# The variance of an encoder's second normalisation: both chunks of squares through TensorE instead of one summed chunk

## What is computed

```python
o = attention(x) @ Wo[l].T + bo[l]
x = _ln(x + o, ln1_g[l], ln1_b[l])
ff = jax.nn.gelu(x @ W1[l].T + b1[l], approximate=False) @ W2[l].T + b2[l]
x = _ln(x + ff, ln2_g[l], ln2_b[l])
# _ln: m = mean(x); v = mean((x - m) ** 2); (x - m) * rsqrt(v + eps) * g + b
```

## Time and profile before

| | |
|---|---|
| median of 3 runs | 932.23 us (931.94, 932.23, 936.35) |
| profiled execution | 932.26 us |
| its span | 930.5 us |
| mean granted TensorE clock | 0.959 of 2.4 GHz |
| encoder loop (five layers) | about 442 to 820 us of the span |

### The profile page before, as it was taken

One profiled execution on the slowest core, in us unless ns is written; L12 is line 12 of the kernel. 1 busy time (PEld: TensorE's weight loads), 2 busy tenths in 40 slices (PEclk: granted clock), 3 DMA queues, 4 the chain that ended last, 5 costly groups with the idle time before them and its releaser, 6 DMA issues.

```text
span 930.5 us, 16226 instructions
## 1 busy us (share of the span) xinstructions
PE 839.1 (90%) x5890; PEld 765.4 (82%) x5890; DVE 661.7 (71%) x1298; ACT 458.1 (49%) x788; POOL 253.8 (27%) x297
## 2 busy tenths in 40 slices
PE   1898689999999999879999998999999999989788
PEld 0676677799999998779898898998988889879556
DVE  6434756848878877477878778787787777875586
ACT  3015323133333333467667676766756766744421
POOL 0000211001111112035435526415524543532232
PEclk9969987999999999889999999999999999997989
DMA  4000019369989981201021011002102102020000
GB/s 166 0 1 1 1 63 369 114 228 311 343 317 317 315 313 37 94 1 35 12 92 34 11 45 52 27 11 90 34 11 90 34 11 90 1 94 1 1 1 27
DMA packets 18289, 88.34 MB, mean 95 GB/s; under 512 B 3120, under 2 KB 7472, under 8 KB 12240
## 3 DMA queue, kind: packets, MB, share of 16 engines
q1 hardware_dynamic: 18256, 87.90, 26.8%
HBM read 85.05 MB, written 2.84 MB: 94 GB/s over the span
## 4 chain that ended last, share of the span: by engine, by line
PE 44%; issue 25%; POOL 17%; DVE 9%; ACT 3%; DMA 1%; SPq 0%; POOLq 0%; DVEq 0%; ACTq 0%
PE bank L992 12%; POOL W_L L1708 6%; PE bank L1029 5%; POOL arena L1686 4%; POOL HF_L L1744 3%; PE bank L763 3%; PE bank L708 3%; PE bank L1135 2%; POOL WQKV_L L1708 2%; PE bank L881 2%; PE bank L1038 2%; PE bank L1309 1%; POOL SQ L1714 1%; PE bank L862 1%; PE bank L717 1%
## 5 line engine op out<-in xcount | busy, mean ns | idle before, releaser
L992 PE MATMUL bank<-arena 128*128 (+1 forms) x1024 | 117.9, 274 | 0.5 <-ACT arena L1442 0.5
L992 PEld LDWEIGHTS bank<-arena 128*128 128x128 f32 x1024 | 117.3, 192 | 0.7 <-ACT arena L1442 0.7
L1686 POOL TENSOR_TENSOR arena<-arena,srec 111x456 f32<-111x456 f32 x56 | 51.8, 953 | 175.1 <-DVE srec L1852 175.1
L763 PE MATMUL bank<-XHL,W_H 128*128 128x296 f32 x384 | 89.7, 312 | 0.0
L763 PE MATMUL bank<-XHL,WQKV_H 128*128 128x296 f32 x288 | 74.0, 331 | 9.0 <-DVE XHL L2188 4.9
L1708 POOL TENSOR_TENSOR W_L<-LW,W_H 128x256 fp32r<-128x256 f32 x96 | 70.1, 768 | 18.9 <-ACT W_H L1502 18.9
L1744 POOL TENSOR_TENSOR HF_L<-arena,HF_H 128x296 fp32r<-128x296 f32 x48 | 43.9, 936 | 114.0 <-ACT HF_H L1603 114.0
L1698 POOL TENSOR_TENSOR QW<-QW,arena x14 | 20.8, 1484 | 180.9 <-DVE arena L2079 110.0
L763 PEld LDWEIGHTS bank<-XHL,W_H 128*128 128x128 f32 x384 | 65.5, 192 | 0.7
L763 PEld LDWEIGHTS bank<-XHL,WQKV_H 128*128 128x128 f32 x288 | 50.0, 196 | 16.1 <-DVE XHL L2188 8.0
L1864 DVE TENSOR_SCALAR OB<-bank,lvec 96x148 f32<-96x148 f32 x144 | 51.2, 368 | 15.6 <-PE bank L833 13.1
(11 more groups left out here) (240 smaller groups left out, 2168.5 us busy)
## 6 DMA issues: line engine op xcount, KB each, us to landing
arena<-ew_in SPq DMA_DIRECT2D x16, 2048.0 KB, 9.1
arena<-ew_in SPq DMA_DIRECT2D x16, 1024.0 KB, 6.8
LW<-lw_in SPq DMA_DIRECT2D x12, 1024.0 KB, 5.0
arena<-route SPq DMA_DIRECT2D x32, 185.0 KB, 3.4
LW<-lw_in SPq DMA_DIRECT2D x6, 768.0 KB, 4.4
fp_weights<-arena SPq DMA_DIRECT2D x1, 2048.0 KB, 6.4
arena<-fp_weights SPq DMA_DIRECT2D x1, 2048.0 KB, 7.3
arena<-patches_in SPq DMA_DIRECT2D x2, 864.0 KB, 6.0
```

What stands on the lines that cost most here:

```text
L763: last = mm(o, w, x, start=(i == 0), stop=(i == len(pairs) - 1))
L992: last = mm(o[:, m * CAP:(m + 1) * CAP], w[:, kc, mi * P:(mi + 1) * P], xg(kc, e), start=(kc == 0), stop=(kc == C - 1))
L1686: nc.gpsimd.tensor_tensor(v, v, srec[0:QROWS, s:s + 2, :].unsqueeze(3).to_broadcast([QROWS, 2, C * JH, KEYS]), ALU.mult).then_inc(p_ready, 1)
```

## The change

In `ln_var_of`, only the first normalisation of a layer (`seq[1] == 0`) waits for POOL's sum of squares and reads one chunk. The second one takes the branch of the other normalisations: it waits until ACT has squared and accumulates over two chunks. POOL's sum for it is gone, and the counts of the semaphore `ln_sqsum` are adapted.

```diff
@@ -695,8 +695,8 @@
             def ln_var_of(seq, h, ones):

                 nch, nt, _, sq = ln_geometry(seq)
-                if isinstance(seq, tuple):
-                    pe.wait_ge(ln_sqsum, seq[0] * 4 + (2 * h + seq[1] + 1))
+                if isinstance(seq, tuple) and seq[1] == 0:
+                    pe.wait_ge(ln_sqsum, seq[0] * 2 + (h + 1))
                     nch = 1
                 elif seq is LN_PATCH:
                     pe.wait_ge(patch_sum, 2 + (h + 1))
@@ -1747,8 +1747,6 @@
                     normalise((x[1] * 2 + (x[0] + 2)) * (HB // 2), HB // 2)
                 else:
                     multiply(0)
-                if y:
-                    add_squares(y[1], 1, y[0])
                 if late_split(x):
                     split_weights(*late_split(x))
```

## The result

In the paired runs behind the prediction the changed kernel took 952.67 us in the median (943.37 to 955.64, six runs) against 933.29 us (931.94 to 938.95, six runs) before: a ratio of 1.0188 with a 95% interval of 1.0147 to 1.0229. So it isn't slower by a fixed amount; in the second series it varies by 25 us where the kernel before varies by 10 us, and why the two series differ stays open. The ratio of 1.0004 reported for the second series leaves out its three slowest executions (943.64, 947.58 and 953.70 us) as a slow state of the chip, but the profile of the last shows the delays of this kernel itself, so I go by the medians and by the profiles.

What follows compares the result with a forecast made beforehand. The loop was taken to go at TensorE's pace. Eleven phases of -0.19 us gave 932.26 - 2.1 + 0.0 = 930.1 us (-0.23%), no difference that can be told; the range for 8 in 10 was 925.5 to 935.5 us.

Steps and rivals of the forecast that it cites:

- The split behind it moves: Query, key and value low halves start earlier, beside VectorE's residual sum: 0.1 us growth, covered or at most 0.5 us.
- The -1.6 us: Whole change if, by the skill's contention rule alone, every such residual sum were fully slowed and on the path.
- The clock: Rival after 834 us: half-clock stretch shorter or none, 925.6 us (chance 0.13), or longer, 934.6 us (0.12).
- The net of TensorE: Second normalisation's variance: start 0.86 us earlier, step 0.67 us longer, -0.19 us per phase, eleven phases -2.1 us.
- The twelfth place: Last phase, where a projection fills the wait: start moves up by 0.68 us, 0.67 us is added, net nothing.
- What hid the twelve sums: GpSimd loses twelve sums of 0.81 us, 9.7 us in all, none on TensorE's path except through the wait.
- The first rival: At the variance loads the start does not move up, products are added: +8.0 us, 940.3 us; chance 0.07.
- Another chain takes over: A wait following VectorE, such as before the projection at 646.64, takes back 0.19 us per phase: 932.3 us; chance 0.17.

Runs made afterwards that it cites:

- the second series: The changed kernel measured again with no edit: median 939.82 us of ten runs, against 934.03 us before.
- the run with the low halves held back: Changed kernel, but GpSimd waits for the second normalisation's squares before making the next low halves: median 937.36 us, before 932.39, ratio 1.0021.

## Why the prediction was wrong

**The step that failed** is in "The split behind it moves": "So it can grow by 0.1 us". I took the longest such sum in the trace, 1.11 us, for the price of one that lies wholly beside GpSimd. But none of them did. The sum at 598.02 ended at 599.02, 0.33 us after the scaling (598.69); the one of 1.10 us at 635.07 ended at 636.17, 0.32 us after its own scaling (632.16 + 3.69 = 635.85). Both ended a third of a microsecond after GpSimd did, less than the 0.47 us that the sum takes alone: they had been held until GpSimd came to an end, or nearly. The row showed how long GpSimd kept on, not how much it slows. Without an end to wait for, the upper bound was the length of the low halves themselves, 4.1 us, and not 0.1. The runs showed 2.05 us more, and 1.9 us of it on TensorE's path. What the trace shows of it in the changed kernel are the single low halves:

```profile
446.13 0.74 POOL L1708 TENSOR_TENSOR WQKV_L<-LW,WQKV_H 128x256 fp32r<-128x256 f32 x1
...
448.17 0.97 POOL L1708 TENSOR_TENSOR WQKV_L<-LW,WQKV_H 128x256 fp32r<-128x256 f32 x1
...
524.93 0.95 POOL L1708 TENSOR_TENSOR WQKV_L<-LW,WQKV_H 128x256 fp32r<-128x256 f32 x1
```

Most pieces take 0.72 to 0.74 us and one in each row 0.95 to 0.97. These rows show one piece each. In the good turn it is the first (524.93), and the sum ends at 525.30; in the bad turn it is the fourth (448.17), and the sum ends at 448.55. The sum is let in at the start of a piece, holds that piece up by 0.23 us, and ends 0.37 or 0.38 us after its start. It was passed over by none, one or three pieces in the runs: 1.00, 1.69, 3.05 us. Why it is held at all these rows don't say; they show when it was let in. The Trainium skill's rule of contention for VectorE instructions with two SBUF inputs (GPSIMD Engine Reference, 1. Specifications) names the right victim, and the traces agree: the sum takes 0.47 us with GpSimd idle and up to 3.06 us beside it. The -1.6 us that I made of it used my wrong price.

**The clock** was the second failure. I had it as a rival for the last phase alone; that the loop had been at 1.00 all along I took as given, and never asked what a wait in it would do. A wait of 1.9 us cost up to 7.5 us by it. In the last phase, where I had looked for it, the edit changed nothing: behind the loop the clock was low for 13.7 us in both profiled executions, before and changed. In the second profile of the changed kernel it lasted 6.8 us, so it varies between executions of one kernel, which is part of the scatter outside the loop.

**The net of TensorE** was right: start up by 0.86, step longer by 0.67, -0.19 us in each phase. The loop of 376.25 us against 378.02 in the run with the low halves held back is -1.77 us over ten places, -0.18 each. The twelfth place, forecast at nothing, costs 0.3 us: from the end of the projection's loads to the next ones it takes 878.90 - (875.05 + 2.21) = 1.64 us, and before 867.71 - 866.36 = 1.35 us. **What hid the twelve sums** was right too: GpSimd has 9.7 us less to do, and the loop is shorter by no more than TensorE's own -0.19 us a phase.

**The first rival**, the start that does not move up, did not come: it moved. Its price was too low as well: kept idle time with six products costs not 8 but 20 us (952.49 us against 932.39), the rest being the clock. So the gain of 0.19 us a phase holds only as long as nothing else makes TensorE wait.

**The other rivals.** "Another chain takes over" named the right kind of event, a VectorE operation held up by GpSimd's weights, at the wrong place and with the wrong size. The 0.97 us at 646.64 were a sample of it already in the trace: the two VectorE operations that it waited for (L2188, from 644.67) took 1.00 and 0.99 us beside the low halves of weights, and 0.52 us where GpSimd was idle.

**The range** (925.5 to 935.5) left this out. Executions at 929 and 934 us occurred, but the median lay above.

## What to carry to other kernels

Whoever takes an instruction out of a queue moves up what stands behind it: look there for a sum of two SBUF operands on VectorE that had its turn only because GpSimd paused. If such an operation ends shortly after GpSimd's work ends, wherever that is, its duration is in part a wait for that end, and its price without the pause is bounded only by the length of what now follows (here it was held by up to three pieces of six). And price a wait in a stretch at full clock by its length plus a possible fall: here 1.9 us stayed 1.9 in one turn of five, and became 3.2 to 3.5 or 7.5 in the others.

## What the runs showed that I had not expected

- One binary, one order of work, two outcomes of the same residual sum within one execution, 1.00 and 3.05 us, though it started 0.28 or 0.29 us after the start of the last scaling piece in both (599.58 - 599.30 and 524.31 - 524.02). What decides isn't settled: three pieces in a row gave 0 long sums in 15 looked at (three profiles), four gave five of 1.69 us, six gave 3 of 5 and 5 of 5 in the changed kernel, 1 of 5 in the kernel before, and twelve of half the width 0 of 5. In all 14 sums that pieces passed by, three pieces were left, counting the one at whose start the sum was let in: it was the second of four or the fourth of six. The rows of three fit that, the normal sums in rows of six and twelve don't. Whether the row, the placement of the code or something else does it, no run here separates.
- What stood ahead of the clock's falls in the loop: 0.88 us of waiting with 1.34 us of one-column products was followed by a fall in nine of ten places, 0.88 with 0.67 and none with 1.34 in none; 2.32 with 0.67 in all four. The busy time alone didn't tell: TensorE counts as busy for 3.30 of 4 us ahead of the fall at 460 us in the kernel before with six products, for 2.54 of 4 ahead of the one at 449 us of the changed kernel, and for 1.93 of 4 at 692 us of its second profile, where no fall came.
